# Zero fills on GpSimd behind every row gather of a graph network's edge passes

## The chip, the cores and the metric

The kernel runs on one core of a Trainium2 chip. The metric is the device time of one execution in microseconds (us), and less is better. Engines are named as the profile names them: PE is TensorE, DVE is VectorE, ACT is ScalarE, POOL is GpSimd, SP is SyncE, which here only issues transfers.

## The reference

A graph has 12,500 nodes with 16 features and 412,500 directed edges sorted by destination. Four layers are applied, each as `x = x + layer(relu(layernorm(x)))`. What costs time is what is done for every edge:

```python
# layer 0: weighted sum of neighbours
out = segment_sum(x[src] * edge_probs[:, None] * weight, dst)
# layer 1: per edge, from edge_attr_8 and a per-node scalar (no gather of rows by src)
m = silu(einsum('ei,ej,ijh->eh', x_j, edge_attr, W_msg_tp)) @ W_msg_lin
# layer 2: one 16x16 matrix per relation type, 90 types
msg = einsum('ei,eio->eo', h[src], W_rel[rel_type]) * e
# layer 3: one 16x16 matrix per edge from a small network, used four times
w = kernel_net(edge_attr).reshape(-1, 16, 16)
for i in range(4):
    agg = segment_sum(einsum('ei,eio->eo', nodes[src], w), dst) * inv_deg
    nodes = gelu(agg + nodes @ root_W[i] + root_b[i])
```

## The kernel before

The edges are padded and laid out as 128 partitions by 3,240 columns, and worked in 270 chunks of 12 columns (1,536 edges). `edge_pass` is called six times, each time over all 270 chunks; these are the gathering passes. Their kinds are `weighted` (layer 0), `relational` (layer 2), `kernel_net` (the first of layer 3's four steps, which also computes the per-edge matrices and writes them to HBM) and three times `kernel_kept` (the other steps, which read those matrices back). Between the first two lies `edge_pass_scatter` (layer 1), which issues its own indirect transfers at L1598 and which the change leaves alone.

In a pass each engine runs its own instruction stream, and semaphores order the streams. Nearly all of a stream is a hardware loop (`Fori`): PE's body (`whole_turns`) holds two chunks; those of POOL, ACT, DVE and SP (`rounds`) hold four in the passes that the steps below speak of, and `kernel_net` has a two-chunk body for PE and ACT.

In a chunk, the rows of the source nodes come in two ways. For `J0` of the 12 columns POOL issues one indirect transfer each (`gather_chunk`, L570): 128 rows of 16 (relational: 32) floats from a table in HBM into the ring buffer `got`, which has four places. `J0` is 8 in `weighted`, 9 in `relational`, 12 in `kernel_net`, 8 in `kernel_kept`. For the other columns the rows are picked by matrix products: ACT makes a one-hot tile `place_hot` (L994), PE multiplies it with the table in 37 matmuls a chunk (L789, `in_place`), DVE masks the result (`picked`, L1106), PE folds it (L804, `in_row`). In `weighted`, DVE also makes 24 small one-hot tiles a chunk (L1089, L1090) for a histogram on PE (L843). In `relational`, PE makes the matrices from one-hot relation types (L864; the one-hot is DVE's L1079). In `kernel_net`, PE and ACT run the two hidden layers (PE L895, L901, L858; ACT L927, L933) and ACT copies the matrices out (`wcopy`, L946). DVE multiplies, reduces and does a segmented scan; the running sums go out by SP.

What sets POOL's order: before chunk k's gathers it waits that the ring place is free (`got_used`, or `rows_made` in `kernel_kept`) and that DVE has copied the indices (`idx_made`, L1097), which DVE does three chunks ahead at the start of its own chunk. The gathers of a chunk are issued one behind the other with nothing between them. No other work runs on POOL in these passes.

Of the kernel before, what the change touches and what calls it, by code (L numbers as in the profile page):

```python
# [30 lines left out]
P = 128  # L31
# [5 lines left out]
C = 12  # L37
# [51 lines left out]
def unique(nc, name):  # L89

    return f"{name}_{nc.next_id()}"
# [24 lines left out]
def build(nc, a, out):  # L116
    with ExitStack() as ctx:
# [85 lines left out]
        layernorm(nc, SB)  # L203
        store_table(nc, h, table16)
        edge_pass(nc, a, SB, "weighted", table16)
        node_slots(nc, SB)
        settle(nc, a, SB, sums16, D, "weighted", table16)
# [8 lines left out]
        relation_rows(nc, SB)  # L216
        store_table(nc, rows, table32)
        edge_pass(nc, a, SB, "relational", table32)
        settle(nc, a, SB, sums32, 2 * D, "relational", table16)
        for depth in range(DEPTH):  # L220
            edge_pass(nc, a, SB, "kernel_kept" if depth else "kernel_net", table16)
            settle(nc, a, SB, sums16, D, "kernel", table16 if depth < DEPTH - 1 else None, depth)
# [331 lines left out]
def rounds(eng, body):  # L554


    for k in range(RING):
        body(k, k, 0, k)
    whole = (CHUNKS - RING + 1) // RING
    with eng.Fori(1, whole) as q:  # L560
        for r in range(RING):
            body(q * RING + r, r, q, None)
    for k in range(whole * RING, CHUNKS):
        body(k, k % RING, k // RING, k)


def gather_chunk(pool, dst, width, table, idx, done, tiles=C):

    for j in range(tiles):
        pool.indirect_dma_start(  # L570
            out=dst[:, j * width:(j + 1) * width], out_offset=None, in_=table,
            in_offset=bass.IndirectOffsetOnAxis(ap=idx[:, j:j + 1], axis=0)).then_inc(done, 16)


def edge_pass(nc, a, SB, kind, table):

    W = 32 if kind == "relational" else 16
# [6 lines left out]
    J0 = C - X  # L584
# [8 lines left out]
    with ExitStack() as ctx:  # L593
        def sb(name, shape, dt=F32):
            return ctx.enter_context(nc.sbuf_tensor(unique(nc, name), shape, dt))

        def ps(name, shape):
            return ctx.enter_context(nc.psum_tensor(unique(nc, name), shape, F32))

        src_at = sb("src_at", [P, T], I32)  # L600
        idx = sb("idx", [P, RING, C], I32)
        got = sb("got", [P, RING, C * W])
        msg = sb("msg", [P, HALVES, F, CW])
# [33 lines left out]
        if kind == "kernel_net":  # L637
# [11 lines left out]
        names = ["weights_in", "first_in", "src_in", "idx_made", "got_in0", "got_in1", "got_in2", "got_in3",  # L649
                 "got_used0", "got_used1", "got_used2", "got_used3", "attr_in0", "attr_in1",  # L650
                 "attr_used0", "attr_used1", "w_made", "w_used", "h1_made", "h1_ready", "h2_made", "h2_ready",
                 "hot_made", "hot_used", "out_made", "stored0", "stored1", "dve_step", "run_cleared", "turn_open", "fetch_open",
                 "place_in0", "place_in1", "range_in0", "range_in1", "places_hot", "in_place_made", "picked_made", "in_row_made", "fetched",
                 "added_clear", "kept0", "kept1", "kept2", "kept3", "mask_made", "scanned", "cleared", "w_copied", "bias_made", "rows_made", "whole_clear", "near_in", "far_in", "whole_step", "near_parts", "far_parts",
                 "w_in0", "w_in1", "w_in2", "w_in3", "w_in4", "w_in5", "w_in6", "w_in7"]
        with phase(nc, *names) as (block, *sems):
            S = dict(zip(names, sems))
            got_in, got_used = ([S[f"{n}{r}"] for r in range(RING)] for n in ("got_in", "got_used"))
# [4 lines left out]
            w_made, w_used, dve_step, out_made = S["w_made"], S["w_used"], S["dve_step"], S["out_made"]  # L663
# [99 lines left out]
            @block.gpsimd  # L763
            def _(pool):
                def chunk(k, r, q, at):

                    if at is None or at >= RING:
                        if kind == "kernel_kept":
                            pool.wait_ge(S["rows_made"], k - RING + 1)
                        else:  # L770
                            pool.wait_ge(got_used[r], q)
                    pool.wait_ge(S["idx_made"], k + 1)

                    pool.sem_inc(S["turn_open"], 1)
                    gather_chunk(pool, got[:, r, :], W, table, idx[:, r, :], got_in[r], J0)

                rounds(pool, chunk)

# [1604 lines left out]
```

## Time and profile before

| | us |
|---|---|
| median of 2 runs | 30095.31 |
| lowest and highest | 30043.46, 30147.17 |
| profiled execution, its own time | 30093.67 |
| its span, first to last instruction | 30091.8 |

Over the span PE is busy 22572.5 us (75%), DVE 17466.6 (58%), ACT 14186.6 (47%) and POOL 18072.7 (60%). The mean granted clock of PE is 0.842 of full speed. No engine is busy throughout, so the time is made of waits as well as of work. In the lists of waits, "issue" stands for time in which an engine waited for nothing that the profile shows. A busy figure of PE counts matmuls whose ends are modelled.

### The profile page before, as it was taken

How to read it: one execution, taken by the hardware profiler on the slowest of the kernel's cores; microseconds unless marked ns; L12 is line 12 of the kernel's file. 1: busy time of each engine (PE TensorE's matmuls, PEld its weight loads, DVE VectorE, ACT ScalarE, POOL GpSimd, SP SyncE). 2: the span in 40 equal slices, each digit the busy share in tenths (PEclk: the TensorE clock that was granted, in tenths of full speed). 3: DMA queues.
4: the chain of work that ended last, by engine and by line, in shares of the span. 5: the costliest groups of instructions: out<-in, count | busy, mean ns of one | idle time of the engine just before them, and what ended most of it. 6: DMA issues, size and time to landing. Idle time of an engine off the chain costs nothing. (4 is left out here: it accounts for less than half of the span.)

```text
span 30091.8 us, 399367 instructions
## 1 busy us (share of the span) xinstructions
PE 22572.5 (75%) x109882; PEld 12540.1 (42%) x109882; DVE 17466.6 (58%) x29340; ACT 14186.6 (47%) x24676; POOL 18072.7 (60%) x17163
## 2 busy tenths in 40 slices
PE   6777748888877778757777776677776878767876
PEld 3333325555545555533333333333333333333333
DVE  4444438888866666653444444466665666656665
ACT  5555521111124444433333333466665666656665
POOL 4555558888865555555555555555555555555555
PEclk8888879999988888877777777788887888878888
DMA  3111125555532222222222222355554555545554
GB/s 88 39 37 38 38 48 94 93 94 92 94 76 62 62 64 62 62 54 85 85 86 86 86 86 85 107 167 167 166 166 137 167 167 168 166 137 166 167 166 136
DMA packets 2201224, 3120.09 MB, mean 104 GB/s; under 512 B 782486, under 2 KB 1548644, under 8 KB 2199460
## 3 DMA queue, kind: packets, MB, share of 16 engines
q1 hardware_dynamic: 1340898, 2927.73, 30.0%
q0 software_dynamic: 790944, 162.36, 8.2%
q10 hardware_dynamic: 69282, 28.92, 0.4%
q8 instruction: 32, 0.52, 0.0%
q14 instruction: 68, 0.56, 0.0%
HBM read 2443.85 MB, written 673.47 MB: 104 GB/s over the span
## 5 line engine op out<-in xcount | busy, mean ns | idle before, releaser
L570 POOL DMA_INDIRECT got<-table,idx x14310 | 13823.7, 966 | 10832.5 <-DVE idx L1097 6364.9
L789 PE MATMUL in_place<-place_hot,tparts 128*128 128x512 fp8e4 (+1 forms) x49950 | 12084.1, 402 | 1891.0 <-issue 1285.9
L994 ACT ACTIVATE place_hot<-place_b,far_lanes 128x512 fp8e4<-128x512 f32 (+1 forms) x17550 | 10587.5, 683 | 27.9 <-DMA added<-rows,add_idx 25.4
L789 PEld LDWEIGHTS in_place<-place_hot,tparts 128*128 128x128 bf16 x49950 | 5199.0, 106 | 8123.6 <-issue 3741.7
L1598 POOL DMA_INDIRECT added<-rows,add_idx x2160 | 3597.6, 1666 | 718.9 <-issue 655.5
L967 ACT ACTIVATE mask<-contw 128x208 f32 (+2 forms) x1350 | 554.5, 411 | 7096.4 <-DMA added<-rows,add_idx 3979.6
L1106 DVE SCALAR_TENSOR_TENSOR picked<-range_b,range_col,in_place 128x512 f32<-128x512 f16 (+1 forms) x1350 | 968.2, 717 | 4251.6 <-DMA added<-rows,add_idx 1438.8
L1215 DVE TENSOR_TENSOR prod<-wcopy,got 128x1024 f32<-128x1024 f32 x810 | 990.9, 1227 | 3243.7 <-ACT wcopy L946 2077.6
L1641 PE MATMUL acc<-hot,spread 128*128 128x392 bf16 x12960 | 2537.4, 350 | 0.0
L1170 DVE TENSOR_TENSOR prod<-w_in,rows_p 128x2048 f32<-128x2048 f32 x810 | 1850.1, 2284 | 1150.2 <-ACT rows_p L982 784.6
L804 PE MATMUL in_row<-fold,picked 128*128 128x16 f32 x8640 | 1163.7, 249 | 1204.9 <-issue 1189.7
L946 ACT ACTIVATE wcopy<-wmat 128x1024 f32<-128x1024 f32 x810 | 828.5, 1023 | 2572.8 <-remote 1580.2
L1224 DVE TENSOR_REDUCE msg<-prod 128x64 f32<-128x1024 f32 x1620 | 1968.1, 1215 | 41.3
L858 PE MATMUL wmat<-k,h 128*128 128x256 f32 x6480 | 1980.4, 435 | 0.0
L901 PE MATMUL h2p<-h,k 128*128 128x512 f32 x1620 | 1121.3, 780 | 1080.3 <-ACT h L927 914.6
L1183 DVE TENSOR_REDUCE msg<-prod 128x128 f32<-128x2048 f32 x810 | 1853.0, 2288 | 105.4
L864 PE MATMUL wmat<-wrel,onehot 90*128 90x256 bf16 x9720 | 1389.7, 287 | 582.4 <-issue 514.0
L804 PEld LDWEIGHTS in_row<-fold,picked 128*128 128x128 f32 x8640 | 1259.5, 198 | 1324.2 <-issue 1166.9
L858 PEld LDWEIGHTS wmat<-k,h 128*128 128x128 f32 x6480 | 1461.4, 226 | 584.9 <-issue 291.3
L1641 PEld LDWEIGHTS acc<-hot,spread 128*128 128x128 bf16 x12960 | 1316.4, 106 | 863.7 <-issue 192.6
L1215 DVE TENSOR_TENSOR prod<-wmat,got 128x1024 f32<-128x1024 f32 x810 | 969.2, 1221 | 1008.7 <-remote 711.2
L864 PEld LDWEIGHTS wmat<-wrel,onehot 90*128 90x128 bf16 x9720 | 977.4, 102 | 974.9 <-issue 758.5
(249 smaller groups left out, 20228.0 us busy)
## 6 DMA issues: line engine op xcount, KB each, us to landing
w_in<-kept SPq DMA_DIRECT2D x2430, 512.0 KB
kept<-wcopy SPq DMA_DIRECT2D x810, 512.0 KB
place_b<-place_row SPq DMA_DIRECT2D x1080, 256.0 KB
got<-table,idx POOLq DMA_INDIRECT x14310
attr<-in_edge_attr SPq DMA_DIRECT2D x270, 768.0 KB
range_b<-range_row SPq DMA_DIRECT2D x1080, 128.0 KB
rows<-in_src_row SPq DMA_DIRECT2D x270, 512.0 KB
sums<-outb SPq DMA_DIRECT2D x1350, 96.0 KB
```

Of the source, the lines that this page charges most:

```text
L570: pool.indirect_dma_start(out=dst[:, j * width:(j + 1) * width], out_offset=None, in_=table, in_offset=bass.IndirectOffsetOnAxis(ap=idx[:, ...
L789: mm = pe.matmul(in_place[b][:, h, :], tparts[:, s, t, :], place_hot[:, b, t, h * XC:(h + 1) * XC], start=(t == 0 and s == 0), stop=(t == ...
L804: mm = pe.matmul(in_row[b][:, j * FW:(j + 1) * FW], picked[:, j * P:(j + 1) * P], fold[:, :], start=True, stop=True)
L858: mm = pe.matmul(wmat[s2][:, j * DD:(j + 1) * DD], weights[:, j * P:(j + 1) * P], moving_parts[0], start=False, stop=True, skip_group_chec ...
L864: mm = pe.matmul(wmat[s2][:, j * DD:(j + 1) * DD], weights[:, j * P:(j + 1) * P], moving, start=(m == 0), stop=(m == len(moving_parts) - 1))
L994: ins = act.activation(place_hot[:, b, t, :], place_b[:, b, :], ACT.Abs_reciprocal_sqrt, bias=SB["far_lanes"][:, t:t + 1], scale=HOT_SLOPE ...
L1170: dve.tensor_tensor(prod_v[:, 0:near, :, :], w_v[:, 0:near, :, :], bcast(rows_p[b].rearrange("p (j f) -> p j f", f=W), 2, D), ALU.mult).th ...
L1183: c.step(dve.tensor_reduce(message_columns(b, 0, near), prod_v[:, 0:near, :, :], AX, ALU.add))
L1215: dve.tensor_tensor(prod[:, s2, :].rearrange("p (j o i) -> p j o i", j=G, o=D), w.rearrange("p (j o i) -> p j o i", j=G, o=D), bcast(rows_ ...
L1224: c.step(dve.tensor_reduce(message_columns(b, g * G, G), prod[:, s2, :].rearrange("p (j o i) -> p j o i", j=G, o=D), AX, ALU.add))
L1598: pool.indirect_dma_start(out=SB["added"][y], out_offset=bass.IndirectOffsetOnAxis(ap=add_idx[:, b, y:y + 1], axis=0), in_=add_rows[:, b, ...
L1641: mm = pe.matmul(acc[c][:, 0:RCOLS], spread[:, b, j, s, :], hot[:, b, j, c * RCOLS:(c + 1) * RCOLS], start=False, stop=False, skip_group_c ...
```

## The change

Each gather is followed on POOL by a `memset` of zeros into its own slice of a new scratch tile `rest` that nobody reads. A slice is 256 float columns wide in `weighted`, 128 in `relational` and `kernel_kept`, 32 in `kernel_net`, over all 128 partitions. The last memset of a chunk raises a semaphore `rested`, and POOL waits for it before the next chunk's gathers. The number, order and operands of the gathers are the same.

```diff
-def gather_chunk(pool, dst, width, table, idx, done, tiles=C):
-
-    for j in range(tiles):
-        pool.indirect_dma_start(
-            out=dst[:, j * width:(j + 1) * width], out_offset=None, in_=table,
-            in_offset=bass.IndirectOffsetOnAxis(ap=idx[:, j:j + 1], axis=0)).then_inc(done, 16)
...
+        rest = sb("rest", [P, {"weighted": 256, "relational": 128, "kernel_net": 32, "kernel_kept": 128}[kind] * J0])
         src_at = sb("src_at", [P, T], I32)
+        RW = rest.shape[1] // J0
...
                     pool.wait_ge(S["idx_made"], k + 1)
 
+                    if at != 0:
+                        pool.wait_ge(S["rested"], k)
                     pool.sem_inc(S["turn_open"], 1)
-                    gather_chunk(pool, got[:, r, :], W, table, idx[:, r, :], got_in[r], J0)
+                    for j in range(J0):
+                        pool.indirect_dma_start(
+                            out=got[:, r, j * W:(j + 1) * W], out_offset=None, in_=table,
+                            in_offset=bass.IndirectOffsetOnAxis(ap=idx[:, r, j:j + 1], axis=0)).then_inc(got_in[r], 16)
+                        ins = pool.memset(rest[:, j * RW:(j + 1) * RW], 0.0)
+                    ins.then_inc(S["rested"], 1)
```

## Rows read from the trace of the kernel before

**Rows 1.** Busy time by windows, one per gathering pass in order (start:end, length, busy).

```profile
105.00:4060.00 3955.00, 2924.84 (x15379) 1481.69 (x15379) 1633.56 (x8091) 2330.74 (x4050) 2055.02 (x2160) 0.85 0.20 47
8827.00:13245.00 4418.00, 3447.16 (x21325) 2251.45 (x21326) 2942.47 (x4325) 2096.60 (x4050) 2365.00 (x2430) 0.85 0.25 63
13407.00:19105.00 5698.00, 4114.72 (x11292) 2174.55 (x11292) 2297.05 (x2969) 1883.63 (x2422) 3283.76 (x3240) 0.78 0.26 85
19264.00:22745.00 3481.00, 2744.59 (x12170) 1335.70 (x12170) 2278.35 (x2182) 2374.92 (x4326) 2048.06 (x2169) 0.87 0.55 166
```

**Rows 2.** Groups by line, POOL, in the windows of weighted, relational, kernel_net, kernel_kept.

```profile
L570 POOL DMA_INDIRECT got<-table,idx x2160 | 2055.0, 951 | 1975.4 <-DVE idx L1097 1347.5 <-issue 627.0 <-DVEq L1155 0.9
...
L570 POOL DMA_INDIRECT got<-table,idx x2430 | 2365.0, 973 | 2167.4 <-DVE idx L1097 1447.5 <-issue 719.2 <-DVEq L1241 0.6
...
L570 POOL DMA_INDIRECT got<-table,idx x3240 | 3283.8, 1014 | 2421.2 <-DVE idx L1097 1464.9 <-issue 956.2
...
L570 POOL DMA_INDIRECT got<-table,idx x2160 | 2039.9, 944 | 1421.0 <-issue 723.6 <-DVE idx L1097 697.4
```

**Rows 3.** PE's waits in weighted (engine, line, releaser: us, times, longest).

```profile
PE hist L843 <- issue: 536.9, 483, 2.6
PE in_row L804 <- issue: 282.9, 278, 2.6
PE in_place L789 <- issue: 229.3, 230, 65.7
```

**Rows 4.** PE's waits in relational, then in kernel_kept, then in kernel_net.

```profile
PE wmat L864 <- issue: 514.0, 579, 2.6
PE in_row L804 <- issue: 226.4, 138, 2.6
PE in_place L789 <- issue: 112.1, 174, 1.8
...
PE in_row L804 <- issue: 303.8, 251, 2.6
PE in_place L789 <- issue: 280.9, 167, 4.7
...
PE h2p L901 <- ACT h L927: 914.6, 126, 25.3
```

**Rows 5.** Timeline of PE in weighted (start, length, instruction, count, idle before).

```profile
2051.20 0.74 PE L804 MATMUL in_row<-fold,picked 128*128 128x16 f32 x6
...
2053.57 0.19 PE L804 MATMUL in_row<-fold,picked 128*128 128x16 f32 x1 [1.25 <-issue]
2059.86 0.24 PE L843 MATMUL hist<-ohq,ohp 128*128 128x98 bf16 x1 [2.54 <-issue]
2065.47 0.67 PE L843 MATMUL hist<-ohq,ohp 128*128 128x98 bf16 x6 [0.46 <-issue]
```

**Rows 6.** Timeline of POOL in that stretch: first and last of 16 gathers.

```profile
2042.88 0.94 POOL L570 DMA_INDIRECT got<-table,idx  x1 [4.36 <-DVE idx L1097]
2044.13 0.94 POOL L570 DMA_INDIRECT got<-table,idx  x1 [0.30 <-issue]
...
2061.65 0.94 POOL L570 DMA_INDIRECT got<-table,idx  x1 [0.30 <-issue]
```

**Rows 7.** Timeline, kernel_kept: last PE step of a stall, last gather of its burst.

```profile
20080.72 3.57 PE L789 MATMUL in_place<-place_hot,tparts 128*128 128x512 fp8e4 x8 [1.51 <-issue]
20077.05 0.94 POOL L570 DMA_INDIRECT got<-table,idx  x1 [0.30 <-issue]
```

**Rows 8.** Timeline, relational: PE's stall, last gather, a gather beside DVE L1079.

```profile
10024.75 0.27 PE L864 MATMUL wmat<-wrel,onehot 90*128 90x256 bf16 x1 [1.77 <-issue]
10037.38 0.59 PE L804 MATMUL in_row<-fold_rel,picked 128*128 128x17 f32 x2 [0.54 <-issue]
10033.51 0.94 POOL L570 DMA_INDIRECT got<-table,idx  x1 [0.30 <-issue]
10015.68 1.30 POOL L570 DMA_INDIRECT got<-table,idx  x1 [0.30 <-issue]
10015.55 0.62 DVE L1079 TENSOR_SCALAR onehot<-types,iota_col 90x1536 bf16<-90x1536 f16 x1 [0.23 <-issue]
```

**Rows 9.** Windows around the stall of rows 5 (clock is the seventh figure).

```profile
2052.10:2065.40 13.30, 1.82 (x8) 0.81 (x7) 0.00 (x0) 0.00 (x0) 8.05 (x9) 0.55 0.08 6
2065.50:2070.00 4.50, 4.50 (x16) 1.91 (x17) 4.20 (x24) 4.29 (x9) 0.00 (x0) 0.50 0.24 74
2073.00:2076.00 3.00, 3.00 (x16) 1.35 (x15) 0.00 (x0) 1.35 (x3) 2.39 (x3) 1.00 0.06 5
```

**Rows 10.** Groups by line, POOL, whole span: its writes to SBUF that are no transfers.

```profile
L254 POOL IOTA iota_i<- 128x1568 int32 x1 | 1.4, 1430 | 0.4 <-PEq L98 0.4
L257 POOL IOTA iota_i<- 128x1 int32 x1 | 0.1, 133 | 10.2 <-DVE iota_b L283 10.2
```

More of the change, by code:

```diff
@@ L651, in edge_pass @@
                  "attr_used0", "attr_used1", "w_made", "w_used", "h1_made", "h1_ready", "h2_made", "h2_ready",
-                 "hot_made", "hot_used", "out_made", "stored0", "stored1", "dve_step", "run_cleared", "turn_open", "fetch_open",
+                 "hot_made", "hot_used", "out_made", "stored0", "stored1", "dve_step", "run_cleared", "rested", "turn_open", "fetch_open",
                  "place_in0", "place_in1", "range_in0", "range_in1", "places_hot", "in_place_made", "picked_made", "in_row_made", "fetched",
```

## The prediction

> **What bounds the kernel now.** I read the windows by pass first, then POOL's groups, then PE's waits, then stretches of the timeline. The six gathering passes take 3955, 4418, 5698 and three times about 3481 us [rows 1] (the other two kept passes differ by under 10 us), 24,514 of the span's 30,092. Over 270 chunks that is 14.65 us a chunk in weighted, 16.36 in relational, 21.10 in kernel_net, 12.89 in kernel_kept. No engine is full: PE has 74% of weighted, 78% of relational, 79% of kept; POOL 52 to 59%.
>
> POOL's floor is the pitch of its gathers. A gather takes 0.94 us and the next starts 1.25 us after it [rows 6]. With each pass's mean duration plus 0.30 [rows 2], a chunk needs 8 x 1.25 = 10.0, 9 x 1.27 = 11.5, 12 x 1.31 = 15.8 and 8 x 1.244 = 9.95 us. So POOL has 4.6, 4.9, 5.3 and 2.9 us a chunk to spare, and it spends them waiting for the indices, DVE's L1097 [rows 2].
>
> PE's lost time has an odd cause. Of weighted's 1030 idle us, 1049 less one start-up wait of 65.7, so 983, are "issue", time in which no semaphore holds PE [rows 3]. In relational it is 514.0 + 226.4 + 112.1 = 853, in each kept pass 585 [rows 4]. The timeline shows where. From 2052 to 2065.4 PE issues one instruction in steps of 0.7 us or multiples (the idle times shown are such steps less a matmul), then six within 0.67 us [rows 5]. POOL meanwhile issues 16 gathers back to back from 2042.88 to 2061.65 [rows 6]. PE recovers 3.8 us after the start of the last gather. In kept the pair is 20080.72 against 20077.05, 3.7 us [rows 7]; in relational 10037.38 against 10033.51, 3.9 us [rows 8]. The stalls differ in length (13, 7 and 14 us) and start at different points of the burst, yet all three end the same time after the burst does. So I read it as: PE's instruction supply is held up while gathers follow each other at 1.25 us, and let go when they pause. After the stall PE also runs at a granted clock of 0.50, its 1.2 GHz level, for at least 4.5 us, and at 1.00, 2.4 GHz, only later [rows 9].
>
> The Trainium skill (Runtime: NRT & Kernel Launch, § Instruction fetch mechanics) says that each sequencer refills its instruction memory in blocks through a DMA queue of its own and that a taken branch outside the held blocks waits for such a transfer. That is a mechanism for a supply that shares the transfer engines with the gathers; no row shows the fetch itself.
>
> **The change, part by part.** Nothing is removed. 14,310 memsets are added: 2160 in weighted, 2430, 3240, and 3 x 2160. The trace has no POOL memset of this size. The nearest rows are the two IOTAs [rows 10]: 1430 ns for 1568 columns, 133 ns for one, so 0.83 ns a column on top of 133. That prices 256 columns at 0.345 us, 128 at 0.24, 32 at 0.16. The lower bound is nothing: the 0.30 us between gathers may be time in which a memset fits. The upper bound is the price plus another such 0.30 us per instruction: 0.645, 0.54, 0.46. I take the middle value, since POOL is one in-order stream and a fill that has no transfer to start has no visible reason for a gap.
>
> New pitches: 1.25 + 0.345 = 1.59; 1.27 + 0.24 = 1.51; 1.31 + 0.16 = 1.47; 1.244 + 0.24 = 1.48. POOL's floor per chunk becomes 12.7, 13.6, 17.7, 11.9 us, all below today's 14.65, 16.36, 21.10, 12.89. So the memsets lie in POOL's waits for indices and cost nothing as long as something else makes the chunk that long. The `rested` wait stands behind the last memset of the chunk before, which the same stream has issued already; behind it on POOL wait only the next gathers, and even a whole gap of 0.30 us a chunk for it (81 us a pass) is within POOL's slack. SP, ACT and PE get no instruction; DVE none.
>
> What the memsets move: they spread the gathers. If the spread lets PE's supply through sooner, stalls shrink. The most that each pass can give is what POOL's new floor leaves: weighted 3955 - 270 x 12.7 = 521 (its stall is 983, so the cap holds), relational 4418 - 3669 = 749 (stall 853), kept 3481 - 3203 = 278 (stall 585), kernel_net 5698 - 4763 = 935. How much of it comes is the open term. At 1.25 us nothing comes through in the three stalls shown, and 3.7 to 3.9 us after the last start it always has; 1.5 to 1.6 us lies in between and nearer to the bad end. I take half of the stall as gone: relational 426. In weighted (490) and kept (290) that half touches the cap, and with chunks of unequal length POOL and PE take turns in bounding, so I take two thirds of the cap: 347, and 3 x 185 = 556. In kernel_net the fill is smallest and PE waits mostly on ACT [rows 4]; I take a fifth of 935, 187. Sum: 347 + 426 + 187 + 556 = 1516. Shorter stalls also mean less time at the half clock, which is in these caps already. From the profiled execution's 30,093.7, which is 2 us under the median: about **28,580 us**, 5% less. Bounds: no release gives nothing; all caps met (521 + 749 + 935 + 834) would be 27,050.
>
> One rule of the skill speaks against the change. In relational a gather beside DVE's L1079 took 1.30 us where others take 0.94 [rows 8], so the two engines do exclude each other for 0.36 us. The Trainium skill (SBUF — State Buffer, § Who interferes with whom) says a DVE operation in a two-port mode and any GpSimd operation lock each other out for a whole instruction, and the trace agrees. By it the 24 tiles of L1089 and L1090 in weighted could wait for two or three memsets of 0.345 us, about 1 us a chunk on an engine that is busy 1634 of 3955 us [rows 1]; the sum would not change.
>
> **The rivals.**
> *The gathers are not spread enough (no release).* For it: in relational the 1.30 us gather makes a pitch of 1.6 in the very burst of the stall, though before it begins, so it decides nothing; and the release needs 3.7 us. Then each stall still ends 3.8 us after the burst, and the burst is longer by the memsets issued during it: weighted has 983 / 13.3 = 74 stalls' worth, times 8 x 0.345 = 2.8 us, 205 us; relational 853 / 14 = 61, times 9 x 0.24 = 2.2, 130; a kept pass 585 / 7 = 84, times five gathers' 1.2, 100, three times; kernel_net perhaps 100. Together 735: about 30,830, slower.
>
> *POOL becomes the bound.* If a memset costs its upper bound, the floors are 8 x 1.89 = 15.1, 9 x 1.81 = 16.3, 12 x 1.77 = 21.2, 8 x 1.78 = 14.3 us a chunk: kept loses 1.4 x 810 = 1130 us, weighted 120. About 31,350. It decides from (12.89 - 9.95) / 8 = 0.37 us per memset in kept.
>
> *Hidden and without effect.* The memset fits in the 0.30 us gap, or release and longer bursts cancel. About 30,050.
>
> **How the numbers follow.** Partial release 0.55, its own range 27,500 to 29,400; hidden or cancelling 0.20; no release 0.16; POOL bound 0.09. Two per cent, about what a measurement of this kernel can tell from no change, is 600 us. Faster needs under 29,490: all but a little of the first case, plus a little of the cancelling one, 0.55. Within 2%: 0.22. Slower: 0.23. The range 27,400 to 31,000 leaves out the POOL-bound case and the tails of the first and of no release, a little under 0.2.
>
> **What would show it.** Right: pitch of gathers 1.5 to 1.6 in weighted; memset rows near 0.3 and 0.2 us; PE's "issue" waits in weighted down from 1049 to about 500 and in relational from 853 to 430; PE's mean clock above 0.85; POOL waiting less for L1097. Wrong at the release: pitch as said, "issue" waits as before or more. Wrong at the price: pitch above 1.75 and POOL's waits for L1097 near zero in kept.

## The result and the profile after

The changed kernel takes 28758.96 us (28730.07 to 28787.84, 2 runs) against 30095.31; the ratio is 0.9582, 95% interval 0.9555 to 0.9608. 28,580 was forecast. The profiled execution's span fell from 30091.8 to 28728.3 us, by 1363.5.

The windows by pass, in the order and with the columns of [rows 1] (window, length, busy time of PE, weight loads, DVE, ACT, POOL, granted clock, share of the transfer engines, GB/s), all six passes of the changed kernel:

```profile
105.00:3465.00 3360.00, 2819.31 (x15367) 1438.11 (x15367) 1718.90 (x8079) 2331.70 (x4049) 2811.28 (x4296) 0.91 0.24 56
8248.00:12480.00 4232.00, 3520.68 (x21318) 2221.11 (x21318) 2951.42 (x4324) 2096.58 (x4050) 2961.22 (x4860) 0.87 0.26 65
12644.00:18090.00 5446.00, 4123.30 (x11280) 2167.93 (x11281) 2298.95 (x2969) 1880.77 (x2420) 3818.18 (x6480) 0.79 0.28 89
18252.00:21605.00 3353.00, 2725.08 (x12154) 1299.04 (x12155) 2284.69 (x2176) 2372.61 (x4321) 2549.00 (x4323) 0.90 0.56 172
21738.00:25095.00 3357.00, 2738.41 (x12161) 1303.40 (x12161) 2280.21 (x2173) 2374.94 (x4324) 2548.88 (x4326) 0.90 0.56 172
25223.00:28590.00 3367.00, 2734.34 (x12152) 1302.49 (x12152) 2283.24 (x2176) 2373.10 (x4321) 2546.61 (x4321) 0.90 0.56 172
```

Weighted gave 3955 - 3360 = 595 us, relational 186, kernel_net 252, the first kept pass 128 (the three together 366, against lengths of 3481, 3475 and 3487 before). Nearly half of the gain is in weighted. PE's busy time in weighted fell too, from 2925 to 2819 us with the same matmuls, and its mean clock rose from 0.85 to 0.91.

POOL's groups in the changed kernel's weighted window (count, busy us, mean ns, idle before), to be set against the first line of [rows 2], and its timeline at two gathers and at the end of a chunk:

```profile
L772 POOL DMA_INDIRECT got<-table,idx x2148 | 2088.4, 972 | 639.6 <-issue 543.9 <-DVE idx L1098 93.9 <-POOL rest L775 1.8
L775 POOL MEMSET rest<- 128x256 f32 x2148 | 727.4, 339 | 1.5
```

```profile
2001.23 0.95 POOL L772 DMA_INDIRECT got<-table,idx  x1 [0.16 <-issue]
2002.18 0.33 POOL L775 MEMSET rest<- 128x256 f32 x1
2002.67 0.95 POOL L772 DMA_INDIRECT got<-table,idx  x1 [0.17 <-issue]
...
2006.51 0.33 POOL L775 MEMSET rest<- 128x256 f32 x1
2007.61 0.95 POOL L772 DMA_INDIRECT got<-table,idx  x1 [0.77 <-issue]
```

The fill starts as the gather ends, and the next gather starts 0.16 us after the fill, where 0.30 us stood between gathers [rows 6]. So 0.14 us of each fill hides in the old gap, and the pitch is 1.44 us. At the end of a chunk 0.77 us stand behind the fill, 0.61 more than elsewhere; the edit adds nothing there but the wait for `rested`, and before the change the 16 gathers of [rows 6] ran over a chunk's end at 0.30. The wait for DVE's indices, 1347.5 us before, is one wait of 93.9 us at the start: POOL now sets the pace of weighted. PE's waits in the same window (engine, line, releaser: us, times, longest), against [rows 3]:

```profile
PE in_place L790 <- ACT place_hot L995: 555.6, 230, 65.6
PE hist L844 <- issue: 8.9, 10, 1.2
PE in_place L790 <- issue: 7.0, 6, 3.0
PE in_row L805 <- DVE picked L1107: 5.6, 1, 5.6
PE in_row L805 <- issue: 0.9, 2, 0.5
```

The 983 us in which PE waited for nothing are 17. What is left is a wait for ACT, which waits for DVE's scan, and DVE for the gathers' data. Relational against [rows 4], then the first kept pass:

```profile
PE wmat L865 <- issue: 215.7, 372, 1.2
PE in_place L790 <- issue: 182.5, 400, 1.2
PE in_row L805 <- issue: 166.5, 268, 2.0
```

```profile
PE in_place L790 <- ACT place_hot L995: 325.5, 86, 110.7
PE in_place L790 <- issue: 288.9, 332, 4.9
PE in_row L805 <- issue: 75.8, 109, 1.9
```

There the hold-up (my name for PE's waits for nothing) is only reduced: 853 to 565 us and 585 to 365. The runs below take relational's part back.

### The profile page after: what moved, and what is told of

Same layout as the page of the kernel before. It is cut to its first block and busy times, and to the rows that moved or that the text cites. A ratio compares the mean times of both kernels' runs of the same rounds, so it can differ in the third digit from the quotient of the medians.

```text
span 28728.3 us, 413713 instructions
## 1 busy us (share of the span) xinstructions
PE 22502.9 (78%) x109882; PEld 12362.4 (43%) x109882; DVE 17590.5 (61%) x29340; ACT 14192.2 (49%) x24676; POOL 21497.8 (75%) x31473
## 5 line engine op out<-in xcount | busy, mean ns | idle before, releaser
L772 POOL DMA_INDIRECT got<-table,idx x14310 | 14075.9, 984 | 6055.7 <-issue 3081.4
L790 PEld LDWEIGHTS in_place<-place_hot,tparts 128*128 128x128 bf16 x49950 | 5100.3, 105 | 9003.7 <-issue 4843.7
L775 POOL MEMSET rest<- 128x128 f32 (+2 forms) x14310 | 3199.8, 224 | 10.2
L805 PEld LDWEIGHTS in_row<-fold,picked 128*128 128x128 f32 x8640 | 1199.7, 197 | 451.1 <-issue 296.4
L1632 PE MATMUL msg<-w_msg,tmp 128*128 128x16 f32 x6480 | 869.9, 267 | 593.2 <-DVE tmp L1755 551.6
```

The lines of the kernel that those rows point to most:

```text
L772: pool.indirect_dma_start(out=got[:, r, j * W:(j + 1) * W], out_offset=None, in_=table, in_offset=bass.IndirectOffsetOnAxis(ap=idx[:, r, j ...
L775: ins = pool.memset(rest[:, j * RW:(j + 1) * RW], 0.0)
L790: mm = pe.matmul(in_place[b][:, h, :], tparts[:, s, t, :], place_hot[:, b, t, h * XC:(h + 1) * XC], start=(t == 0 and s == 0), stop=(t == ...
```

## The experiments

The question was whether the gain comes from the distance between the gathers, and whether the gathers are what holds PE up. The runs came on chips of two kinds, and this has to be said first because nothing below can be read without it: beside the first four runs and beside the last two the kernel before took 29,890 and 29,941 us, beside the other six 23,974 and 23,986. Each ratio is against the kernel before on the same chip. I call the first kind held-up chips, the second free chips. The recorded pair belongs to the first. None of these chips appears on two occasions, so whether the kind belongs to the chip or to the occasion is not shown.

### One column (held-up chip)

```diff
-        rest = sb("rest", [P, {"weighted": 256, "relational": 128, "kernel_net": 32, "kernel_kept": 128}[kind] * J0])
+        rest = sb("rest", [P, 1 * J0])
```

> Every fill of the changed kernel is cut to one column; its instructions, the added semaphore and its wait all stay. Spacing theory: a one-column fill (about 0.13 us) vanishes in the 0.30 us gap, the pitch of the gathers stays 1.25 us, PE's waits for nothing (issue) in weighted come back to about 1000 us and the time to 30,100 (within 150). Rival, that the added instructions, the semaphore or the longer GpSimd stream bring the gain: time stays near 28,760.

Measured: 30001.46 us, ratio 1.0031 (1.0020 to 1.0042). The fill takes 128 ns and vanishes in the gap; the pitch is 1.25 us. PE's waits in weighted:

```profile
PE hist L844 <- issue: 437.4, 419, 2.0
PE in_place L790 <- issue: 313.0, 308, 65.2
PE in_row L805 <- issue: 210.9, 217, 2.6
```

Less one start-up wait of 65.2 these are 896 us, against 983 before and 17 in the changed kernel. The instructions, the semaphore, its wait (the 0.77 us at a chunk's end is here too) and the longer POOL stream bring nothing, and cost 0.3%. In weighted, then, the gain comes with the width of the fills. Relational says something else. It takes 4190 us here at 1.25 us, 42 less than in the changed kernel at 1.34, and PE waits for nothing no longer than its 565 us:

```profile
PE wmat L865 <- issue: 272.7, 324, 1.9
PE in_place L790 <- issue: 235.8, 288, 2.5
```

Kernel_net takes 5718 us, against 5698 before and 5446 in the changed kernel.

### One partition (held-up chip)

```diff
-                        ins = pool.memset(rest[:, j * RW:(j + 1) * RW], 0.0)
+                        ins = pool.memset(rest[0:1, j * RW:(j + 1) * RW], 0.0)
```

> The fills keep their widths but write one partition instead of 128. Spacing theory: the duration of a fill depends on its columns, so the pitches stay at 1.44, 1.34, 1.26 and 1.34 us and the time at 28,760 (within 150). Rival, that what matters is the writing of 128 partitions through the port shared with VectorE: time moves back towards 30,100 with the pitches unchanged.

Measured: 29548.81 us, ratio 0.9874 (0.9827 to 0.9921), between the two expectations. The premise was off by a little: POOL's group in weighted is

```profile
L775 POOL MEMSET rest<- 1x256 f32 x2160 | 680.9, 315 | 0.9
```

315 ns instead of 339, so the pitch is 1.42 us and not 1.44; in relational and kernel_kept it is about 1.31 and not 1.34. Weighted took 3395 us, close to the 3360 of the changed kernel, although PE's waits for nothing there are 433 us, in pieces of about half a microsecond; the kept passes took about 3480, as before, relational 4419 and kernel_net 5647, against 4232 and 5446 in the changed kernel. Two causes fit: a small loss of distance matters much near 1.3 to 1.4 us, or the writing of 128 partitions has a part. This run doesn't part them.

### One fill per chunk (held-up chip)

```diff
-                        ins = pool.memset(rest[:, j * RW:(j + 1) * RW], 0.0)
+                    ins = pool.memset(rest[:, :], 0.0)
                     ins.then_inc(S["rested"], 1)
```

> The same columns are filled, but by one fill behind the last gather of a chunk (2048 columns in weighted, about 1.8 us; 1152 in relational, 384 in kernel_net, 1024 in kernel_kept); inside a chunk the gathers follow each other at 1.25 us. Theory A, that every gap between gathers must be a little longer: stalls of 9 to 13 us return, time about 30,000. Theory B, that one long pause is as good as many short ones: PE is let go at every chunk end, weighted near 3,450 us, relational and kernel_kept in between; time 29,000 to 29,500.

Measured: 28818.85 us, ratio 0.9631 (0.9567 to 0.9694), which is the changed kernel's gain. POOL's timeline: one fill of 1.82 us and a gap of 0.77, then gathers 1.25 us apart.

```profile
1998.40 1.82 POOL L775 MEMSET rest<- 128x2048 f32 x1
2001.00 0.95 POOL L772 DMA_INDIRECT got<-table,idx  x1 [0.77 <-issue]
2002.26 0.95 POOL L772 DMA_INDIRECT got<-table,idx  x1 [0.30 <-issue]
```

Weighted took 3388 us, relational about 4060, kernel_net about 5380, kernel_kept about 3435. Theory A, that every gap must be longer, falls. A pause in each chunk frees PE too, though not wholly: of its issue waits in weighted 468 us are left, and of the first kept pass's 514 against 585. Theory B gave 29,000 to 29,500; the gain was larger.

### 512 columns everywhere (held-up chip)

```diff
-        rest = sb("rest", [P, {"weighted": 256, "relational": 128, "kernel_net": 32, "kernel_kept": 128}[kind] * J0])
+        rest = sb("rest", [P, 512 * J0])
```

> All fills 512 columns wide, about 0.55 us, in all six passes. Pitch about 1.66 us. Spacing theory: PE's issue waits fall near zero in every pass, but GpSimd bounds: 8 x 1.66 = 13.3 us a chunk in weighted and kernel_kept, 9 x 1.68 = 15.1 in relational, 12 x 1.7 = 20.4 in kernel_net; passes of about 3600, 4150, 5600 and 3600 us. Time about 29,300. If issue waits in relational stay above 300 us, the spacing is not what frees PE there.

Measured: 31157.78 us, ratio 1.0412 (1.0366 to 1.0458). Slower, as the second rival (POOL becomes the bound) had it, and yet PE hardly waits for nothing in any pass. Its issue waits in relational and in the first kept pass:

```profile
PE in_row L805 <- issue: 21.2, 82, 0.4
PE wmat L865 <- issue: 9.8, 3, 3.8
```

```profile
PE in_place L790 <- issue: 49.5, 14, 4.8
```

The pitch is 1.66 us. With the changed kernel this gives, on held-up chips, relational 853 us of such waits at 1.25 (509 with one column, 533 in a second trace, below), 565 at 1.34, 31 at 1.66; kernel_kept 585, 365, 50; weighted 983 at 1.25, 17 at 1.44, 14 at 1.66. What is gained is paid on POOL: weighted takes 3754 us, relational 4357, kernel_net 5946, the kept passes 3793. My 29,300 was too low because a chunk took more than its gathers' pitch: 3754 / 270 = 13.9 us in weighted against 8 x 1.66 = 13.3. The 0.61 us at the chunk's end is the difference.

### 256 columns everywhere, twice, and 192 (free chips)

```diff
-        rest = sb("rest", [P, {"weighted": 256, "relational": 128, "kernel_net": 32, "kernel_kept": 128}[kind] * J0])
+        rest = sb("rest", [P, 256 * J0])
```

A further run has 192 in place of the 256, and 128 in kernel_net.

> 256 columns behind every gather in all six passes: pitch 1.45 us everywhere. Weighted stays as in the changed kernel (about 3340 us). Theory, that 1.45 us is the pitch at which PE's supply comes through: PE's issue waits fall below 150 us in relational (564 in the changed kernel) and kernel_kept (364). GpSimd's floor is then 9 x 1.45 = 13.1 us a chunk in relational, 17.4 in kernel_net, 11.6 in kernel_kept. Relational near 3,850 us, kernel_kept near 3,250, kernel_net 5,200: total near 28,100. Rival, that the pass and not the pitch decides: relational and kernel_kept stay within 2% of the changed kernel, total 28,700.

> 192 columns in weighted, relational and kernel_kept, 128 in kernel_net: pitches near 1.40 us and 1.34 us. If release grows evenly with the pitch, weighted has about 200 to 300 us of issue waits left, relational about 400, kernel_kept about 200. If there is a threshold between 1.42 and 1.45 us, weighted's issue waits are above 400 us, as in the run with one partition (429 at 1.42).

> 256 columns behind every gather in all passes. Where the hold-up is (before near 30,000): PE's issue waits vanish in relational and kernel_kept as they do in weighted, total 27,900 to 28,200, below the changed kernel. Where it is not (before near 24,000): GpSimd bounds every pass at 1.45 us a gather, 27,830 as in the last run, the same time in both cases, because then nothing but GpSimd's pitch sets it.

Measured: 27834.60 and 27823.01 us with 256 columns, ratios 1.1612 (1.1578 to 1.1645) and 1.1600 (1.1567 to 1.1634); 26946.39 with 192 and 128 in kernel_net, ratio 1.1241 (1.1209 to 1.1272). The kernel before took 23,974 and 23,986 us beside them. In none of the six passes does PE wait for nothing, so neither expectation on thresholds can be judged from them; on a held-up chip only 512 columns were run beyond the changed kernel's widths. They price the pitch: the more columns, the longer.

### A double fill behind every second gather (free chip)

```diff
+                        if j % 2 == 1 or j == J0 - 1:
-                        ins = pool.memset(rest[:, j * RW:(j + 1) * RW], 0.0)
+                            ins = pool.memset(rest[:, (j - j % 2) * RW:(j + 1) * RW], 0.0)
```

> The same columns are filled, but one double-width fill stands behind every second gather: the distances alternate between 1.25 and about 1.66 us in weighted, 1.25 and 1.45 in relational and kernel_kept. The mean pitch is that of the changed kernel. Theory, that the longest recurring gap counts: weighted keeps issue waits near zero and relational and kernel_kept gain (gap 1.45): total about 28,500. Theory, that the mean pitch counts: all as in the changed kernel, 28,760.

Measured: 26449.63 us, ratio 1.1034 (1.1002 to 1.1066). On such a chip there is no hold-up to free, so it says nothing on which gap counts; it costs what the changed kernel costs there (26,318, below).

### The changed kernel again (free chip)

> The changed kernel beside a new set of runs of the kernel before. In the last four runs the kernel before took 23,974 us instead of 29,890 and no PE instruction waited for nothing, so the hold-up was not there to be freed. Theory, that the fills pay only where the hold-up is: if the kernel before takes about 30,000 here, the ratio is 0.955 to 0.965 again; if it takes about 24,000, the changed kernel is slower, by GpSimd's added time: 8 x 0.20 us a chunk in weighted, 9 x 0.09 and 8 x 0.09 in the others where GpSimd bounds, about 24,900, ratio 1.03 to 1.05.

Measured: 26318.37 us against 23986.42, ratio 1.0973 (1.0941 to 1.1005). The same kernel that is 4% faster on one chip is 10% slower on another. Its first four passes there:

```profile
105.00:3462.00 3357.00, 2814.15 (x15379) 1437.06 (x15379) 1713.81 (x8084) 2331.87 (x4049) 2806.89 (x4303) 0.91 0.24 56
8234.00:11753.00 3519.00, 3032.21 (x21303) 2075.34 (x21304) 2935.60 (x4316) 2097.55 (x4049) 2950.88 (x4853) 0.98 0.32 78
11924.00:16384.00 4460.00, 3814.74 (x11276) 2042.59 (x11276) 2291.41 (x2968) 1918.94 (x2419) 3762.37 (x6445) 0.89 0.34 109
16556.00:19667.00 3111.00, 2642.15 (x12150) 1292.77 (x12150) 2273.02 (x2172) 2401.94 (x4320) 2544.26 (x4320) 0.90 0.60 186
```

Weighted is the same on both kinds, 3357 and 3360 us: with 256 columns nothing of the hold-up is left, and POOL's sequence alone sets it. The others are not: 3519 against 4232, 4460 against 5446, 3111 against 3353. So in the recorded run the changed kernel still pays 713 + 986 us and 745 in the three kept passes, 2444 together, to the hold-up. POOL has no slack here either; in kernel_kept it waits 18.2 us for indices; its "issue" waits are the gaps of 0.16 and 0.77 us:

```profile
POOL got L772 <- issue: 547.6, 2152, 1.7
POOL got L772 <- DVE idx L1098: 18.2, 2, 14.2
```

My expectation of 24,900 left the chunk's end out. The change added 2332 us. An estimate from the measured distances: the pitch grew by 0.19, 0.09, 0.01 and 0.09 us, about 1,200 us over the 14,310 gathers, and the 0.61 us at 1,620 chunk ends is another 990. That makes 2,200 if POOL bounds the kernel before as well; the kernel before has no trace from such a chip, so this last is not shown.

The hold-up is not PE's alone. In kernel_net it is DVE above all that waits for nothing. The lines are, in turn, of the kernel before, the changed kernel on the held-up chip and the changed kernel on the free one:

```profile
DVE prod L1215 <- issue: 1137.6, 192, 27.4
DVE prod L1216 <- issue: 1061.9, 175, 26.5
DVE prod L1216 <- issue: 34.6, 5, 8.2
```

### Few gathers, on both kinds

From the kernel before, with no fills. It leaves out every gather of a chunk but the first, so its sums are not those of the graph. The last line stands for four waits for gathers that are changed alike:

```diff
-                    gather_chunk(pool, got[:, r, :], W, table, idx[:, r, :], got_in[r], J0)
+                    if at is not None and at < RING:
+                        pool.memset(got[:, r, 0:J0 * W], 0.0).then_inc(S["rested"], 1)
+                        pool.wait_ge(S["rested"], at + 1)
+                    gather_chunk(pool, got[:, r, :], W, table, idx[:, r, :], got_in[r], 1)
...
-                        dve.wait_ge(got_in[r], q * (16 * J0))
+                        dve.wait_ge(got_in[r], q * (16))
```

> The kernel before, without any fill, in which only the first column of each chunk is gathered; the rows of the other columns are left as they are, so their sums are not those of the graph. Every other instruction of PE, ACT, DVE and SP stays. If gathers in close succession hold up PE's instruction supply, its issue waits fall from 982, 851 and 583 us in weighted, relational and kernel_kept to below 50 us each. If the supply is held up by PE's own loop or by the other transfers, they stay within a third of that. Time without the hold-ups: weighted about 3,250, relational 3,650, kernel_kept 3,050 a pass; total near 27,000.

> Only the first column of each chunk is gathered (the sums of the other columns are not those of the graph), no fill. On the faster chip this took 22,180 us with no issue waits. If this call's kernel before takes about 30,000: theory, that the gathers in close succession hold up PE's supply, gives issue waits below 50 us a pass and a time near the 22,180 of the other chip; the rival, that the supply on such a chip is slow whatever GpSimd does, leaves hundreds of us of issue waits and a time above 26,000. If the kernel before takes 24,000, it is 22,180 again.

Measured: 22179.76 us on a free chip, ratio 0.9253 (0.9226 to 0.9280), and 22182.18 on a held-up one, ratio 0.7412 (0.7390 to 0.7434). Two chips that differ by 6,000 us with the gathers agree within 3 us without seven eighths or more of them. The first run was no test of the hold-up, which its chip did not have; the second was. The 27,000 was 4,800 us too high, because it took off only the stalls: without the gathers weighted takes 2558 us, of which PE is busy 2524. On the held-up chip, the first four passes and PE's waits in weighted:

```profile
105.00:2663.00 2558.00, 2524.43 (x15391) 1367.62 (x15391) 1613.24 (x8116) 2332.95 (x4051) 255.60 (x274) 1.00 0.24 67
7420.00:10572.00 3152.00, 2891.26 (x21314) 2062.01 (x21314) 2902.72 (x4322) 2098.40 (x4050) 256.11 (x274) 1.00 0.27 76
10737.00:14292.00 3555.00, 3506.17 (x11295) 1924.14 (x11296) 2295.03 (x2970) 1917.96 (x2423) 343.58 (x274) 0.97 0.34 130
14449.00:16890.00 2441.00, 2391.26 (x12152) 1229.60 (x12152) 2255.85 (x2176) 2369.73 (x4321) 256.06 (x275) 0.99 0.71 230
```

```profile
PE in_place L792 <- ACT place_hot L997: 64.8, 1, 64.8
PE hist L846 <- DVE ohq L1093: 6.9, 2, 4.2
```

PE, with the same loops and the same transfers by SP, has no issue waits there and runs at a clock of 1.00. This shows the cause of the hold-up: the gathers. It is neither PE's loop nor the other traffic: all transfers together move 230 GB/s in the kept pass here against 166 before. The rival of a slow supply whatever POOL does is out. That it is their close succession and not their number is the 512-column run's to show, which has every gather and no hold-up.

### The kernel before again (held-up chip)

> The kernel before itself, for its profile on the chip that this call gets. If its time is near 24,000: no PE instruction waits for nothing in weighted, relational and kernel_kept (issue below 50 us a pass against 982, 851 and 583), the pitch of the gathers is 1.25 us as before, and the passes take about 2,850, 3,200 and 2,700 us. If its time is near 30,000 the trace repeats the recorded one.

Measured: 29916.53 us, ratio 0.9995 (0.9983 to 1.0007), on a held-up chip, so the trace of a free one is missing. It shows something else, how much one pass varies between two such traces. Weighted and relational:

```profile
105.00:4035.00 3930.00, 2919.43 (x15333) 1467.64 (x15334) 1623.16 (x8057) 2329.89 (x4049) 2055.70 (x2160) 0.85 0.20 47
8815.00:12871.00 4056.00, 3445.65 (x21311) 2270.14 (x21312) 2941.74 (x4318) 2096.43 (x4049) 2381.51 (x2430) 0.88 0.27 68
```

Weighted is within 25 us of [rows 1], relational 362 us shorter than its 4418, and shorter than the changed kernel's 4232. Its issue waits there are 533 us, fewer than the changed kernel's 565, where the recorded trace had 853; in the first kept pass they are 627 against 585. So the 186 us that relational gave in the recorded pair, and the 4060 us with one fill per chunk, lie within what that pass varies by without any change. The gain of weighted, 595 us, does not, nor does kernel_net's: that pass took 5698, 5749 and, with one column, 5718 us, and 5446 in the changed kernel.

## Why the prediction was right, step by step

**What bounds the kernel.** The reading of the stalls held in the main. That gathers in close succession hold up PE was argued in the prediction from three stalls that ended 3.7 to 3.9 us after the last gather's start; the few-gathers run on the held-up chip and the 512-column run show it. That the clock comes back with it held too: 0.85 to 0.91 in weighted, 1.00 without gathers. The fixed time after the burst is no rule, though: a stall from 1346 us on ended by 1351 while the gathers went on, after one gap of 1.83 us between two of them. That what is held up is PE's instruction supply stays a reading. The refill of instruction memory by transfers, which the prediction names as a mechanism, is not borne out: between 260 and 4030 us, where 950 of weighted's 983 us of such waits lie, the kernel before has one packet of the kind "instruction":

```profile
q14 instruction: 1, 0.01, 0.0%
```

**The price of a fill.** Forecast 0.345, 0.24 and 0.16 us for 256, 128 and 32 columns from the two IOTAs [rows 10]; measured 0.339, 0.22 to 0.23 and 0.143. What the fill adds to the pitch was mis-sized: I added the whole price (1.59, 1.51, 1.47, 1.48), but 0.14 us of it hides in the gap that I had named as the lower bound. Measured 1.44, 1.34, 1.26, 1.34. The truth lay between the value taken and the lower bound; the upper bound, and with it the price of the rival in which POOL becomes the bound, fell. The sign "pitch of gathers 1.5 to 1.6 in weighted" did not come.

**What a pitch makes of a chunk.** Here the error went the other way. With 1.44 us weighted's floor would be 11.5 us a chunk, and a chunk took 12.4, though POOL waited for no one. The prediction gave the `rested` wait at most a gap of 0.30 us a chunk, "within POOL's slack", and left it out of the floors. Measured, a chunk's end costs 0.61 us, and in weighted POOL has no slack left to hide it: 8 x 1.44 + 0.61 = 12.1. The rest is longer gathers (mean 972 ns against 951) and a few longer gaps. That the wait makes the 0.61 us is concluded from the edit; no run leaves the wait out. The two errors nearly cancel against the 12.7 forecast, which is luck.

**The release.** I took half of the hold-up. In weighted it was all (983 to 17 us), in kernel_kept 38% (585 to 365), and in relational a third by the recorded pair (853 to 565), none by the second trace of the kernel before (533) or by the one-column run (509). By pass: weighted 595 us for 347, relational 186 for 426, kernel_net 252 for 187, kept 366 for 556; sum 1399 for 1516, and 36 us went back outside the passes. The total is nearer than its terms, which miss by +248, -240, +65 and -190: luck again. Weighted beat even its cap of 521, because the cap stood on the overlong pitch. Relational's term was too high and its sign is not secured. kernel_net, with a pitch raised by hardly 0.01 us, can hardly have gained by spacing as I described it; its 252 us are not explained by any run here.

**The rule against the change.** DVE's operations in weighted do wait for the fills. The two groups of one-hot tiles in the changed kernel, against the kernel before, whose two lines stand first:

```profile
L1089 DVE TENSOR_SCALAR ohp<-iota_b,srange 128x128 bf16<-128x128 bf16 x3231 | 828.0, 268 | 40.8 <-issue 40.6
L1090 DVE TENSOR_SCALAR ohq<-iota_b,splace 128x98 bf16<-128x98 bf16 x3230 | 823.3, 266 | 52.2 <-issue 51.9
...
L1091 DVE TENSOR_SCALAR ohq<-iota_b,splace 128x98 bf16<-128x98 bf16 x3226 | 1032.0, 353 | 0.0
L1090 DVE TENSOR_SCALAR ohp<-iota_b,srange 128x128 bf16<-128x128 bf16 x3227 | 1016.3, 367 | 0.0
```

DVE's busy time in weighted rose by 85 us, 0.3 us a chunk where I allowed 1, and DVE does not set the pace. That is the exclusion which the Trainium skill (SBUF — State Buffer, § Who interferes with whom) states, and the trace agrees with it as far as the tiles get longer beside the fills. The fill's duration alone does not set by how much: DVE is busy 1635.65 us in weighted with one column (128 ns), and 1642.33 with 256 columns on one partition, although those fills take 315 ns, nearly the 339 of the changed kernel; the tiles take 288 and 300 ns there. Why one partition disturbs DVE less, no run here shows.

**The rivals.** No release: out, on a held-up chip. POOL bound: true of weighted already, and of everything with 512 columns. Hidden and without effect: what a fill of one column is. What no rival had is that the hold-up is there on one chip and not on another. The forecast holds for chips of the kind that it was made from, and has the wrong sign on the others: there the second half of its argument, "the memsets lie in POOL's waits for indices", fails, because those waits were made by the hold-up (the changed kernel waits 18.2 us for indices in kernel_kept there and 309.6 on the held-up chip; of the kernel before there is no trace).

## What to carry to other kernels

When an engine idles for "issue" in long runs of single instructions, look at what POOL's gathers do at that moment, and whether the stalls end soon after the burst does; pausing the gathers can pay although nothing on the path is removed. Slack that comes from a stall is not slack: price an addition also for the case that the stall is absent, and time it on more than one chip, since here the same edit was 4% faster and 10% slower. The gathers' own cost is larger on a held-up chip, 7,760 us against the 1,336 gained, and 1,790 on a free one: without most of them both chips tried need 22,180 us. And on an engine with no slack even a wait for its own last instruction is to be priced: here 0.61 us a chunk.

## What the runs showed of the hardware

- Two kinds of chip for one program: the kernel before at 29,890 to 30,095 us or at 23,974 to 23,986, with nothing between, and the same 22,180 us on both once most gathers are gone. What makes a chip (or an occasion) the one or the other stays open.
- PE's waits for nothing against the pitch of gathers on held-up chips, in kernel_kept: 585 and 627 us at 1.25, 542 at 1.31 (one partition), 365 at 1.34, 50 at 1.66; none to speak of at 1.25 alternating with longer gaps, or at 1.34 and 1.44, on free ones. By which resource the gathers hold the other engines up, no run here shows.
- A GpSimd fill of 1, 32, 128, 256 and 512 columns takes 128, 143, 222, 339 and about 545 ns, and lengthens the distance of two gathers by its duration less 0.14 us; on one partition instead of 128 the 256 columns still take 315 ns. From the last fill of a chunk to the next gather, with the wait for the fill's semaphore between them, it is 0.77 us instead of 0.16.
